# Attention scores on 64-row halves of the array, with the maxima's copies split over two queues

## The reference

```python
q = q * cos + rotate_half(q) * sin
k = k * cos + rotate_half(k) * sin
scale = 1.0 / jnp.sqrt(jnp.asarray(HD, x.dtype))      # HD = 8
attn = jnp.einsum('bhqd,bhkd->bhqk', q, k) * scale
attn = jax.nn.softmax(attn, axis=-1)
out = jnp.einsum('bhqk,bhkd->bhqd', attn, v)
```

## Time and profile before

| | |
|---|---|
| runs shown | 907.14, 909.83, 907.4 us; median 907.4 us |
| the profiled execution | 907.05 us, of which its span is 905.3 us |
| before the first score product (L1640) | 0 to 43.5 us |
| the maxima's lead | 43.5 to 69.2 us |
| passes 0 to 7 | 69.2 to 418 us |
| later stages | to 905.3 us |
| busy share of the span | DVE 88%, PE 86%, ACT 76%, POOL 27% |

### The profile page before, as it was taken

How to read it: one execution, slowest core, us unless ns; L and a number is a source line. 1 busy time by engine, 2 the same in 40 slices (tenths; PEclk the granted TensorE clock), 3 DMA queues, 4 the chain that set the end, 5 groups by cost and what they waited for, 6 DMA issues and landing times.

```text
span 905.3 us, 12616 instructions
## 1 busy us (share of the span) xinstructions
PE 779.2 (86%) x4297; PEld 414.1 (46%) x4312; DVE 794.6 (88%) x752; ACT 686.4 (76%) x1298; POOL 239.9 (27%) x136
## 2 busy tenths in 40 slices
PE   7789999999999999999666677677575899999998
PEld 3312222212122122225445556666575688888886
DVE  5998899998899899997997979999999887888765
ACT  2406888888788788886557799999998578888884
POOL 3800000000000000010001357898986701422000
PEclk9958999999999999999798788999998899999999
DMA  5313132312122220011001334565554202222101
GB/s 136 89 46 100 50 107 69 106 53 74 36 81 67 65 60 13 13 40 47 0 1 25 118 122 149 181 218 187 186 174 149 89 24 71 94 71 70 56 37 47
DMA packets 41467, 75.16 MB, mean 83 GB/s; under 512 B 7588, under 2 KB 25324, under 8 KB 40764
## 3 DMA queue, kind: packets, MB, share of 16 engines
q1 hardware_dynamic: 41404, 74.36, 26.0%
HBM read 64.71 MB, written 8.31 MB: 81 GB/s over the span
## 4 chain that ended last, share of the span: by engine, by line
PE 50%; DVE 27%; ACT 11%; issue 9%; POOL 2%; DMA 0%; DVEq 0%; ACTq 0%; POOLq 0%
PE ps L1680 9%; PE ps L1707 9%; DVE nmax_k L1240 7%; PE ps L1969 6%; PE ps L1970 6%; PE ps L1971 6%; ACT dtb L1075 5%; PE ps L1651 4%; DVE hst L1409 4%; DVE nmax L1237 3%; ACT abar L1049 2%; PE ps L1867 2%; PE ps L1913 2%; PE ps L1790 1%; ACT prob L937 1%
## 5 line engine op out<-in xcount | busy, mean ns | idle before, releaser
L937 ACT ACTIVATE prob<-ps 128x512 f32<-128x512 f32 x512 | 272.5, 599 | 90.4 <-PE ps L1680 88.4
L1240 DVE TENSOR_REDUCE nmax_k<-ps 128x2 f32<-128x1024 f32 x224 | 262.3, 1219 | 28.2 <-PE ps L1651 27.0
L1680 PE MATMUL ps<-qs,ks 96*128 96x512 bf16 x512 | 159.4, 387 | 3.9 <-ACT prob L937 2.6
L862 POOL TENSOR_TENSOR hc<-hst,cbr 128x1024 f32<-128x1024 f32 x63 | 151.2, 2422 | 43.3 <-DVE hst L1409 22.7
L1409 DVE TENSOR_TENSOR_SCAN hst<-abar,ps 128x1024 f32<-128x1024 f32 x64 | 142.8, 2272 | 4.4 <-issue 1.9
L1707 PE MATMUL ps<-prob,vq 128*16 128x512 f32 x1024 | 134.6, 597 | 0.1
L1523 DVE TENSOR_TENSOR act_l<-act_t,act_h 128x1024 fp32r<-128x1024 f32 x64 | 91.8, 1444 | 34.5 <-ACT act_h L1172 34.5
L1075 ACT ACTIVATE dtb<-dtxt,bt 128x128 f32<-128x128 f32 x352 | 107.4, 394 | 2.9 <-PE ps L1867 2.9
L1680 PEld LDWEIGHTS ps<-qs,ks 96*128 96x128 bf16 x512 | 34.0, 97 | 153.0 <-ACT prob L937 121.7
L1168 ACT ACTIVATE act_t<-ps,b1t 128x512 f32<-128x512 f32 x128 | 81.8, 681 | 25.3 <-PE ps L1971 25.2
L1867 PE MATMUL ps<-ident,dtb 128*128 128x128 f32 x352 | 54.6, 303 | 45.7 <-DVE hst L1409 37.2
(11 more groups left out here) (221 smaller groups left out, 1125.1 us busy)
## 6 DMA issues: line engine op xcount, KB each, us to landing
cbr<-s_dram SPq DMA_DIRECT2D x64, 512.0 KB, 3.9
gate<-c_dram SPq DMA_DIRECT2D x5, 1024.0 KB, 4.7
qs<-q_dram SPq DMA_DIRECT2D x16, 288.0 KB
ks<-k_dram SPq DMA_DIRECT2D x48, 96.0 KB
o_dram<-o_sb SPq DMA_DIRECT2D x14, 256.0 KB, 2.4
gate<-c_dram SPq DMA_DIRECT2D x6, 512.0 KB, 4.0
wf<-in_L_ffn_w SPq DMA_DIRECT2D x8, 256.0 KB, 5.0
wfq<-in_L_ffn_w SPq DMA_DIRECT2D x8, 256.0 KB, 4.9
```

The costliest lines, as they stand in the source:

```text
L862: nc.gpsimd.tensor_tensor(hc[:, m % RING], hst[:, m % RING], cbr[:, m % RING], ALU.mult).then_inc(s_hc, 1)
L937: nc.scalar.activation(prob[:, n % 8], ps[:, 4 + (first + n) % 3], ACT.Exp, scale=ATT_SCALE).then_inc(s_exp, 1)
L1240: nc.vector.tensor_reduce(nmax_k[:, half, kk, 2 * pair:2 * pair + 2, qt], ps[:, 2 * pair:2 * pair + 2, :], AX.X, ALU.max, negate=True).the ...
L1680: nc.tensor.matmul(ps[:, 4 + (first + n) % 3], ks[p][:, kt // 4, j, kt % 4 * P:(kt % 4 + 1) * P], qs[p][:, half, j, :], start=True, stop=T ...
```

## The change

The kernel after it keeps six of the nine pairs of parts (`PAIRED`), 48 rows a head, and two rows for the maxima: 50 rows. Heads 0 and 2 lie at partitions 0 to 49, heads 1 and 3 at 64 to 113. The six copies of each part are laid out in DRAM already, so that they are stored two times over, and each stack comes back with 8 transfers a pass, `km` and `qm` with 4. On SP the parts of the first batch entry are stored as each part is ready, and head groups 1 to 3 each one pass ahead of their use. The parts of the second entry are stored by GpSimd, 24 transfers in passes 0 and 1. The maxima of heads 1 and 3 are copied by GpSimd (four transfers, `s_prow`), those of heads 0 and 2 by SP (four transfers, 16 partitions each instead of 32). The fill rows and their transfers are gone; GpSimd sets all of `ks` to one instead.

```diff
-PROD = PARTS * PARTS * HD
-ROWS = 96
+PAIRED = ((0, 2), (0, 0), (0, 1), (1, 0), (1, 1), (2, 0))
+COPIES = tuple(tuple(slice(r[0], r[-1] + 1, r[1] - r[0] if len(r) > 1 else 1) for r in
+                     ([n for n, pair in enumerate(PAIRED) if pair[kind] == part] for part in range(PARTS))) for kind in range(2))
+PROD = len(PAIRED) * HD
+ROWS = PROD + 2
+SIDE = 64
 ATT_SCALE = 1.0 / float(np.sqrt(np.float32(HD)))
 VW = 16
...
         prob = sb("prob", [P, 8, BANK])
@@ -215,8 +217,8 @@
...
+        def side(h, rows=ROWS):
+            return slice(SIDE * (h % 2), SIDE * (h % 2) + rows)
+        def maxima_rows(p, half, n, z):
+            return qs[p][SIDE * n + PROD:SIDE * n + ROWS, half].rearrange("r h (q t) -> r (h q) t", t=P)[:, :, 32 * z:32 * z + 32]
+        def copies_of(u, part, group):
+            c, kind = PIECES[u]
+            dst = (q_dram, k_dram)[kind][4 * (c // 2) + group, c % 2, COPIES[kind][part]]
+            src = part_rows(u, slice(QC * group, QC * (group + 1)))[:, part].unsqueeze(1)
+            return dst.rearrange("n c t -> c n t"), src.to_broadcast([QC, dst.shape[0], BANK])
+        def copy_to(u, copy, groups):
+            c, kind = PIECES[u]
+            dst = (q_dram, k_dram)[kind][4 * (c // 2) + groups.start:4 * (c // 2) + groups.stop, c % 2, copy]
+            return dst, part_rows(u, slice(QC * groups.start, QC * groups.stop))[:, PAIRED[copy][kind]]
...
-        LOADS = 16 * 2 * (PARTS + 1)
-        HEAD_LOADS = 16 * 2 * 3 * QUAD
+        LOADS = 16 * 2 * 2 * 2
+        HEAD_LOADS = 16 * 2 * 2
+        STORES = 16 * PARTS
...
-            def store_parts(u, groups):
-                c, kind = PIECES[u]
-                sp.wait_ge(s_part3, u + 1)
-                dst = (q_dram, k_dram)[kind]
-                for g in groups:
-                    sp.dma_start(dst[4 * (c // 2) + g, c % 2].rearrange("n c t -> c n t"),
-                                 part_rows(u, slice(QC * g, QC * g + QC))).then_inc(s_parts_out[u], 16)
+            def store_part(u, part, group=0):
+                sp.wait_ge((s_part1, s_part2, s_part3)[part], u + 1)
+                sp.dma_start(*copies_of(u, part, group)).then_inc(s_parts_out[u], 16)
+            def store_group(group):
+                for u in range(CHUNKS):
+                    for part in range(PARTS):
+                        store_part(u, part, group)
+            def group_stored(group):
+                for u in range(CHUNKS):
+                    sp.wait_ge(s_parts_out[u], STORES * (group + 1))
             def load_heads(it, p, f):
-                for h in range(QUAD):
-                    q, k = (t[bass.ds(it, 1), f].rearrange("o n (d h) t -> (o n d) h t", h=QUAD)[0:2 * HD, h]
-                            for t in (q_dram, k_dram))
-                    sp.dma_start(km[p][32 * h:32 * h + 32, f], k.unsqueeze(0).to_broadcast([2, 2 * HD, BANK])).then_inc(s_qm[p], 16)
...
-            def load_q(it, p, f, done):
-                sp.dma_start(qs[p][0:PROD, f], q_dram[bass.ds(it, 1), f].rearrange(
-                    "o n (d h) t -> (o n d) (h t)", h=QUAD).unsqueeze(1).to_broadcast([PARTS * HD, PARTS, QUAD * BANK])).then_inc(done, 16)
-            def load_k(it, p, f, done):
-                for a in range(PARTS):
-                    sp.dma_start(ks[p][HD * PARTS * a:HD * PARTS * (a + 1), f], k_dram[bass.ds(it, 1), f].rearrange(
-                        "o n (d h) t -> d (o n) (h t)", h=QUAD)).then_inc(done, 16)
+                for t, to in ((k_dram, km), (q_dram, qm)):
+                    sp.dma_start(to[p][:, f], t[it, f, 1:5].rearrange("n (d h) t -> h (n d) t", h=QUAD)).then_inc(s_qm[p], 16)
+            def load_stack(stack, dram, it, f, done):
+                for n in range(2):
+                    sp.dma_start(stack[side(n, PROD), f], dram[it, f].rearrange(
+                        "n (d h m) t -> m (n d) h t", d=HD, m=2)[n]).then_inc(done, 16)
...
-                    sp.dma_start(
-                        qs[p][PROD:PROD + 2, half].rearrange("n h (q t) -> n (h q) t", t=P)[:, :, 32 * z:32 * z + 32],
-                        nmax_t[32 * z:32 * z + 32, half, :]).then_inc(s_nrow[half], 16)
+                    sp.dma_start(maxima_rows(p, half, 0, z), nmax_t[32 * z:32 * z + 16, half, :]).then_inc(s_nrow[half], 16)
...
-            sp.wait_ge(s_fill, 1)
-            fill_set(0)
-            store_parts(0, (0,))
-            store_parts(1, (0,))
-            sp.wait_ge(s_parts_out[0], 16)
-            sp.wait_ge(s_set[0], 32)
-            load_q(0, 0, 0, s_first)
-            store_parts(2, (0,))
...
+            for u, part in ((0, 0), (1, 0), (0, 1), (2, 0), (0, 2), (1, 1), (1, 2)):
+                store_part(u, part)
+            sp.wait_ge(s_parts_out[0], STORES)
+            load_stack(qs[0], q_dram, 0, 0, s_first)
+            store_part(2, 1)
+            sp.wait_ge(s_parts_out[1], STORES)
+            sp.wait_ge(s_set[0], 1)
+            load_stack(ks[0], k_dram, 0, 0, s_first)
+            store_part(2, 2)
+            for part in range(PARTS):
+                store_part(3, part)
+            sp.wait_ge(s_parts_out[2], STORES)
+            load_stack(ks[0], k_dram, 0, 1, s_first)
+            sp.wait_ge(s_parts_out[3], STORES)
+            load_stack(qs[0], q_dram, 0, 1, s_second_half)
+            store_group(1)
+            store_maxima(0, 0, 0)
+            group_stored(1)
             load_heads(1, 1, 0)
-            store_maxima(0, 0, 0)
             load_heads(1, 1, 1)
-            sp.wait_ge(s_set[1], 32)
+            sp.wait_ge(s_set[1], 1)
             load(1, 1)
-            for u in range(CHUNKS):
-                store_parts(u, (2, 3))
-            for u in range(CHUNKS):
-                sp.wait_ge(s_parts_out[u], 16 * QUAD)
             def one_pass(it, p, more, again=None, meanwhile=None):
                 store_maxima(it, p, 1)
+                if it == 0:
+                    store_group(2)
+                    group_stored(2)
                 if it + 2 < PASSES:
...
-                sp.wait_ge(s_set[2], 32)
+                sp.wait_ge(s_set[2], 1)
                 load(2, 2)
-            def store_second_batch():
+                store_group(3)
...
+                    sp.wait_ge(s_parts_out[u], 2 * STORES)
...
-            nc.gpsimd.memset(fill[:, 0], 0.0)
-            nc.gpsimd.memset(fill[:, 1], 1.0).then_inc(s_fill, 1)
+            nc.gpsimd.memset(ks[0][:], 1.0).then_inc(s_set[0], 1)
...
+            def store_maxima(it, p, half):
+                pool.wait_ge(s_nmax, 2 * it + half + 1)
+                for z in range(4):
+                    pool.dma_start(maxima_rows(p, half, 1, z), nmax_t[32 * z + 16:32 * z + 32, half, :]).then_inc(s_prow[half], 16)
+            def store_piece(u):
+                pool.wait_ge(s_part1, u + 1)
+                pool.wait_ge(s_part2, u + 1)
+                pool.wait_ge(s_part3, u + 1)
+                for copy in range(len(PAIRED)):
+                    pool.dma_start(*copy_to(u, copy, slice(0, QUAD))).then_inc(s_parts_out[u], 16)
...
-            with pool.Fori(1, PASSES // SETS) as r:
-                for p in range(SETS):
-                    pool.wait_ge(s_pv, STEPS * (SETS * (r - 1) + p + 1))
...
+            for n in range(1, SETS):
+                nc.gpsimd.memset(ks[n][:], 1.0).then_inc(s_set[n], 1)
+            store_maxima(0, 0, 0)
+            for it in range(PASSES):
+                if it < 2:
+                    store_piece(CHUNKS + 2 * it)
+                store_maxima(it, it % SETS, 1)
+                if it < 2:
+                    store_piece(CHUNKS + 2 * it + 1)
+                if it + 1 < PASSES:
+                    store_maxima(it + 1, (it + 1) % SETS, 0)
+                if it + SETS < PASSES:
+                    pool.wait_ge(s_pv, STEPS * (it + 1))
+                    values(it + SETS, it % SETS)
...
-                    nc.vector.tensor_copy(nmax_p[:, 0:16], nmax[:, half]).then_inc(s_mstep, 1)
+                    high, low = (nmax_p[:].rearrange("p (m n h q) -> p n h m q", m=2, n=2, h=2)[:, n] for n in range(2))
+                    both = nmax[:, half].rearrange("p (h m q) -> p h m q", h=2, m=2)
+                    nc.vector.tensor_copy(high, both).then_inc(s_mstep, 1)
                     dve.wait_ge(s_mstep, w + 2)
-                    nc.vector.tensor_tensor(nmax_p[:, 16:32], nmax[:, half], nmax_p[:, 0:16], ALU.subtract).then_inc(s_mstep, 1)
+                    nc.vector.tensor_tensor(low, both, high, ALU.subtract).then_inc(s_mstep, 1)
                     dve.wait_ge(s_mstep, w + 3)
                     dve.wait_ge(s_nrow[half], 64 * it)
+                    dve.wait_ge(s_prow[half], 64 * it)
...
-                mm = nc.tensor.matmul(ps[:, 2 * (t % 2) + kk], qs[p][:, half, h, q * P:(q + 1) * P],
-                                      ks[p][:, kk, h, :], start=True, stop=True)
+                mm = nc.tensor.matmul(ps[:, 2 * (t % 2) + kk], qs[p][side(h, PROD), half, h // 2, q * P:(q + 1) * P],
```

(52 more changed lines are left out.)

21 lines of the change are left out of this document (3 added, 18 removed).

## The result

| kernel | median us (runs) | ratio to before, 95% interval |
|---|---|---|
| before, beside it | 907.6 (14) | 1 |
| after | 904.84 (14) | 0.9953 (0.9935 to 0.9971) |

The change makes the kernel 0.5% faster where 2.3% was forecast. The profiled span went from 905.3 to 903.9 us, 1.4 less, where the medians differ by 2.8: the profiled execution after (905.71) is 0.9 slower than its median. The time lies at the upper end of the range, but the forecast itself was wrong: nearly all of the gain that was counted on is missing.

What follows compares the result with a forecast made beforehand. A two-step loop of 5.22 us through VectorE's reductions and PE's products, not PE alone, was taken as the bound. Terms -21.6 - 1.1 + 1.2 + 0.6 = -20.9 against 907.4 gave 886.5 us, range 876 to 905.

Steps and rivals of the forecast that it cites:

- thirteen half passes: Passes 0 to 7: each half pass falls from 21.68 to 20.14 us, 1.54 less; fourteen of them were forecast at -21.6.
- half pass from 128.45: Pass 1's second half, one of the fourteen half passes: 1.54 us less like the others.
- first half pass (steps, first copies): Pass 0: five steps before 85.78 gain 1.1 us; the first wait for maxima's copies costs 1.2.
- SP late in pass 4: SP's queue, kept until 260.46 by pass 6's weights and set: maxima's copies start 1.8 us late, priced at 0.6.
- before the first transposed maxima, after the last: Lead before pass 0, paced by 22 reductions, and pass 7's rest, at 2.39 us a step: no change.
- The step that failed: Stores and loads: SP issues 22 transfers a pass instead of 42; doubled stored bytes delay nothing except in pass 0.
- The steps: Passes 0 to 7: score products side by side save 0.44 us per two steps, so steps go from 2.61 to 2.39.
- rival E: Clock falls because PE streams less; a step at half clock needs about 3.5 us, 20 such eat the gain; slower 0.03.
- X: GpSimd's time for one transfer of the maxima's copies, taken as 1.0 us; four are covered up to that.
- rivals A and B: Maxima's copies: A, slow GpSimd transfers, partial loss 0.10, near break-even 0.03, slower 0.10; B, reductions block them, 894.9 us, 0.04.
- The estimate with the Trainium skill's figure: Maxima's copies: about 1 us to first byte on GpSimd's path, 0.6 on SP's, giving 1.06 a transfer, sum 3.6 higher.
- Rivals C and D: C: array halves don't overlap, steps stay 2.61, 907 to 909 us, 0.05. D: reductions become only bound, 875 us, 0.07.

Runs made afterwards that it cites:

- the first two experiments: Two separate edits of the changed kernel, maxima ahead and GpSimd's stores later: 896.40 and 895.85 us.
- maxima ahead: Changed kernel; in pass 1 SP copies the second half's maxima before waiting for stored group 3 and loading pass 3's set: 896.40 us.
- GpSimd's stores later: Changed kernel with GpSimd's six-store pieces of pass 1 moved behind the maxima they stood in front of: 895.85 us.
- neighbours on one half: Kernel with maxima ahead, heads in the order 0, 2, 1, 3, so a pair's two score products lie on one array half: 995.46 us.
- all copies by SP: Kernel with maxima ahead, all eight transfers of the maxima issued by SP, none by GpSimd: 920.81 us.
- 64 rows: Kernel with maxima ahead, each head's products over 64 rows instead of 50, zeros of qs meeting ones of ks: 889.62 us.
- the late start: GpSimd zeros the first set's qs before its ks, delaying PE's warm-up products; with 64 rows 889.6 us, against 892.3 with the early start.

## Why the prediction was wrong

The terms of its sum, against the two profiled executions (us):

| term | forecast | measured |
|---|---|---|
| thirteen half passes | -20.0 | -14.9 |
| half pass from 128.45 | -1.5 | +11.0 |
| first half pass (steps, first copies) | +0.1 | +2.5 |
| SP late in pass 4 | +0.6 | 0 |
| before the first transposed maxima, after the last | 0 | -0.45, +0.47 |
| sum | -20.8 | -1.4 |

**The step that failed** is the one on stores: "Bytes stored double, but nothing waits for them except in pass 0, where groups 1 to 3 are stored in 5 us pieces between waits that have 20 us each." Two things in it are false. Group 3 is stored last in pass 0's turn of the queue, behind the load of the third set, and its stores, its landing, an output and a load of a set stand in front of pass 1's second maxima. And 5 us holds only where SP is alone (5.77 with GpSimd's stores moved away, 11.99 beside them). I had priced what GpSimd's own transfers cost GpSimd, not what its 24 stores do to the other queue. Either edit takes most of the 12.5 us of this term back, as the first two experiments show: the half pass fell from 32.82 us to 20.60 with the maxima ahead, and to 21.83 with GpSimd's stores later.

**Half passes.** The steps came out: 2.39 on average, two in 4.79, by the overlap alone (neighbours on one half). Mis-sized was what a half pass gets of it: the eleven that nothing disturbed went from 21.54 to 20.30, 1.23 less and not 1.54. I took all eight steps at 2.61 and gave the rest to the half's end. In truth two of them were at 2.38 before and can't fall, and the one with VectorE's small operations is VectorE's own, in both kernels (3.42 before, 3.41 after): it reduces without a pause there, three reductions in 3.47 us, as the timeline of DVE after shows:

```profile
202.10 3.47 DVE L1271 TENSOR_REDUCE nmax_k<-ps 128x2 f32<-128x1024 f32 x3
```

The other five gain 1.3 together. Of the 5.1 us that are missing in this term, 3.6 are twelve times 0.3; the other 1.5 is the half pass of pass 4, 22.45 before and 22.43 after, where a dip of the clock behind ACT's pause made a step 3.36 us long. Without a dip there, as with the maxima ahead, it takes 21.58, so 0.85 of the 1.5 is the clock's.

**First half pass.** Its copies cost nothing (first exponential at 69.49, before 70.34). But the clock rose at 82.3 instead of 73.4, so two steps took 4.47 and 4.50 instead of 2.77 and 2.81. That is rival E, which had 0.03, in a place that I had not looked at: I had asked whether a full clock would fall, not whether it would rise as soon. How much of the 2.5 us belongs to the change stays open: fewer rows go with a later rise, but the same instructions also gave 87.2 and 87.4, and a rise of the kernel before at 77.2 needed only a shift of its start.

**Maxima's copies.** Four take 2.23 us, X = 0.56 and not 1.0, and they land 1.7 us after their issue in the median (1.7 to 2.3; the traces have no landing of SP's). With that X rivals A and B fall: the copies were covered, and reductions that fill nine tenths of VectorE's time don't hold GpSimd's transfers off. The estimate with the Trainium skill's figure (DMA: Bandwidth & Descriptors, Specifications), X = 1.06, was as far off as mine; the nearest row, SP's 0.66, would have done. Splitting the copies was worth more than its price says: with all copies by SP the time is 24 us longer, lost where SP is late.

**Rivals C and D** are excluded by the steps: neither 2.61 nor 2.28. SP's lateness in pass 4 cost nothing visible, and pass 7's rest and the later stages were unchanged, as said.

## What to carry to other kernels

When work is moved in one queue, list for every wait behind it what now stands in front, with the slack of that one wait; and where a second queue starts to move data, time the first queue's issues beside it, not alone. When a change makes matrix products smaller or puts them side by side, look at the granted clock of the kernel in its slowest stretches first: fewer rows can cost more than the overlap gains, and filling the tile with zeros added nothing to the passes here. The best version here needs both: maxima ahead of stores, 64 rows, 889.6 us (2.1% under before, where the change alone gave 0.5%); 2.7 us of it come with the late start, which is luck.

## What the runs showed of the hardware

- The granted clock depends on the rows of the array that products use, at equal instructions and columns: 50 rows stayed at 1.2 GHz for 225 us after 1.0 us of idle PE, 64 rows kept 2.4 GHz behind one of 0.8 (995.5 against 908.8 us). Which property of the rows it is (their number, or that a tile is full) was not separated, and the start differed too.
- The instructions alone don't fix its course: with equal ones up to there the rise in pass 0 came at 82.3, 87.2 and 87.4 us, and executions of the kernel before had mean granted clocks from 0.931 to 0.949.
- Zero-weight products over 128 rows, without a gap for 15 us, didn't raise it.
- A transfer's issue on SP, 0.46 us for these stores, takes up to 2.5 us, and a load's 3.8, while GpSimd has six stores of 128 KB in flight (medians of 5.5 to 5.9 us from issue to landing); with none in flight, one load's issue still took 2.0.
- GpSimd issues a small transfer in 0.56 us and a 128-row store in 0.69, also while VectorE reduces.
